# Wider products that carry the low-rank rows with the values, and the first outputs' load at the head of the last pair

## The reference

```
h = x @ W.T + b + 2 * (x @ A[i]) @ B[i]         # A: 1024 x 16, B: 16 x 1024, i per sequence
q, k, v = h @ w_q, h @ w_k, h @ w_v             # bs 8, 32 query heads, 8 key and value heads of 32
o = softmax(q k.T / sqrt(32)) v ;  x = x + o @ w_o
y = x @ weight[j].T                             # j per sequence
x = x + sum over the best 2 of 4 experts of gate * 4 * (y @ A_e.T) @ B_e.T
```

## Time and profile before

| | |
|---|---|
| runs | 1053.78, 1052.08, 1053.18 us |
| profiled execution | 1050.59 us, of it the span 1048.9 us |
| busy | PE 97%, PE weight loads 78%, DVE 60%, ACT 43%, POOL 22% |
| mean granted TensorE clock | 0.988 |
| weight folding ends, first pair begins | 162.5 us |
| score groups of step 0, pairs 1 to 4 | 183.5, 312.6, 447.0, 582.4 us |

### The profile page before, as it was taken

One profiled execution on the slowest core, in us unless ns is written; L12 is line 12 of the kernel. 1 busy time (PEld: TensorE's weight loads), 2 busy tenths in 40 slices (PEclk: granted clock), 3 DMA queues, 4 the chain that ended last, 5 costly groups with the idle time before them and its releaser, 6 DMA issues.

```text
span 1048.9 us, 17421 instructions
## 1 busy us (share of the span) xinstructions
PE 1013.4 (97%) x6934; PEld 820.2 (78%) x6934; DVE 633.5 (60%) x1071; ACT 449.5 (43%) x782; POOL 234.0 (22%) x224
## 2 busy tenths in 40 slices
PE   7999999999999999999999999999899999999997
PEld 6878787877678776787767787676589998988986
DVE  6562724667856578664776657654665655655653
ACT  5121223355754557554665556635422332323321
POOL 1000001123323233223332246643111111111100
PEclk9999999999999999999999999999999999999998
DMA  7030312111421124211232134453966756766531
GB/s 263 0 101 1 131 47 73 27 38 43 123 55 38 29 56 122 60 40 27 53 113 60 42 93 142 123 154 142 257 215 197 229 193 199 228 196 205 201 122 40
DMA packets 49888, 117.41 MB, mean 112 GB/s; under 512 B 7298, under 2 KB 26114, under 8 KB 45712
## 3 DMA queue, kind: packets, MB, share of 16 engines
q1 hardware_dynamic: 40080, 81.70, 26.4%
q0 software_dynamic: 9728, 34.61, 10.4%
HBM read 86.38 MB, written 18.89 MB: 100 GB/s over the span
## 4 chain that ended last, share of the span: by engine, by line
PE 90%; DMA 3%; DVE 3%; ACT 1%; SPq 1%; issue 1%; POOL 0%; ACTq 0%
PE psP L759 20%; PE psW L1043 17%; PE psF L254 11%; PE psG L1071 8%; PE psO L825 6%; PE psT L812 5%; PE psS L801 5%; PE psP L774 4%; PE psX L1286 3%; PE psO L829 2%; PE psY L1305 2%; PE psF L265 1%; DMA x_raw<-in_xT 1%; PE psM L836 1%; PE psP L740 1%; PE psP L742 1%
## 5 line engine op out<-in xcount | busy, mean ns | idle before, releaser
L673 DVE TENSOR_REDUCE nmax<-psS 128x2 f32<-128x512 f32 x256 | 164.5, 684 | 153.8 <-PE psS L801 152.1
L550 POOL TENSOR_TENSOR p_sum<-probs 128x512 f32<-128x512 f32 x128 | 167.6, 1310 | 372.6 <-ACT probs L600 372.3
L759 PE MATMUL psP<-x_hl,wq 128*128 128x512 f32 x960 | 235.1, 392 | 0.6 <-DVE q_stack L653 0.6
L759 PEld LDWEIGHTS psP<-x_hl,wq 128*128 128x128 f32 x960 | 175.2, 189 | 32.8 <-issue 0.8
L1043 PE MATMUL psW<-wq 128*128 128x256 f32 x1536 | 196.7, 283 | 1.6 <-DVE q_stack L653 1.2
L1043 PEld LDWEIGHTS psW<-wq 128*128 128x128 f32 x1536 | 190.3, 191 | 6.2 <-issue 1.3
L600 ACT ACTIVATE probs<-psT 128x512 f32<-128x512 f32 x256 | 139.2, 596 | 54.4 <-PE psT L812 53.9
L1052 ACT ACTIVATE cond_hi<-cond_raw 128x1024 fp32r<-128x1024 f32 x64 | 66.8, 1057 | 152.5 <-PE psG L1071 148.1
L1056 DVE TENSOR_TENSOR cond_lo<-cond_raw,cond_hi 128x1024 fp32r<-128x1024 f32 x64 | 78.3, 1235 | 89.1 <-ACT cond_hi L1052 89.0
L812 PE MATMUL psT<-q_stack,k_stack 98*128 98x512 f32 x256 | 90.1, 427 | 7.7 <-ACT probs L600 5.4
L653 DVE TENSOR_TENSOR q_stack<-psP,q_stack 32x512 fp32r<-32x512 f32 x128 | 87.8, 686 | 9.2 <-ACT q_stack L566 7.1
(11 more groups left out here) (122 smaller groups left out, 1252.8 us busy)
## 6 DMA issues: line engine op xcount, KB each, us to landing
cond_raw<-in_cond POOLq DMA_DIRECT2D x64, 512.0 KB, 4.1
x_raw<-in_xT SPq DMA_DIRECT2D x32, 256.0 KB, 3.9
q_stack<-q_stack SPq DMA_DIRECT2D x32, 256.0 KB, 3.1
o_scratch<-o_sb SPq DMA_DIRECT2D x64, 128.0 KB
o_raw<-rden_scratch SPq DMA_DIRECT2D x32, 256.0 KB, 5.4
o_raw<-o_scratch SPq DMA_DIRECT2D x8, 1024.0 KB, 8.8
x_sb<-in_xT SPq DMA_DIRECT2D x8, 1024.0 KB, 6.8
outT<-x_sb SPq DMA_DIRECT2D x32, 256.0 KB, 2.5
```

The source lines that it names most:

```text
L550: pool.tensor_tensor(p_sum[:, heads], probs[:, 0, heads], probs[:, 1, heads], ALU.add).then_inc(sum_done, 1)
L673: dve.tensor_reduce(nmax[:, n % 2, 2 * hp:2 * hp + 2, qt], psS[:, i % 2].rearrange("p (h k) -> p h k", h=2), AX.X, ALU.max, negate=True).t ...
L759: mm = pe.matmul(out, wq[:, i, w, k * P:(k + 1) * P], x[:, k, part], start=(k == 0 and n_ == 0), stop=False)
```

## The change

The low-rank factor A moves from `a_stack` into the moving side of the v products: `v_hi` holds for each k 32 columns of A (high and low half) of one sequence, 256 of the value weights and 32 of the other sequence, and a v unit's three products per k have 288, 272 and 256 columns. The 32 extra columns are x @ A per token; VectorE adds their two halves into `u_tok`, the unit "t" turns four such tiles with TensorE, and ScalarE and VectorE make `u_stack` from it. The values' own low-rank product can't be the v unit's last any more, so the units "r0" and "r1" multiply it into two further banks and VectorE adds it to `v_sb`, which is held twice. The blocks of the weights, `WORK` and `SEQ` are rearranged: all v units of a pair lie in steps 13 and 14 of the pair before. The x rows are split three in step 11 and five in step 12 by ScalarE, three in step 12 and five in step 13 by VectorE. The load of the first outputs is issued at the end of the step ahead of the last pair, multiplied in its step 0, and split in steps 1 and 2. Buffers are moved in SBUF for all of this, and the last tiles of the weight folding are taken out by two instructions each.

```diff
-BLOCKS = ["k0", "q0", "q1", "q2", "v0", "v1", "q3", "k1", "q4", "q5", "q6", "q7"]
+BLOCKS = ["k0", "q0", "q1", "q2", "q3", "k1", "q4", "q5", "q6", "q7", "v0", "v1"]
+VB = BLOCKS.index("v0")
+VC = NKV + 4 * R
+V0 = 2 * R
...
+                units = range(CB * j, CB * (j + 1))[:VB - CB * j]
+                ins = nc.scalar.activation(wq[:, units[0]:units[-1] + 1, 0, m * P:(m + 1) * P],
+                                           psF[:, bank(j, m), 0:P * len(units)].rearrange("p (u c) -> p u c", c=P), ACT.Copy)
+                if j == CHUNKS - 1:
+                    ins = nc.scalar.activation(v_hi[:, m, V0:V0 + NKV], psF[:, bank(j, m), P * len(units):512], ACT.Copy)
+                ins.then_inc(tile_hi, 1)
...
+                if j == CHUNKS - 1:
+                    ins = dve.tensor_tensor(v_lo[:, m], psF[:, bank(j, m), P * len(units):512],
+                                            f(v_hi[:, m, V0:V0 + NKV]), ALU.subtract)
+                ins.then_inc(tile_lo, 1)
...
 WORK = [
-    (["v0"], ["q2:0-4"]),
-    (["q2:4-6"], ["q2:6-8"]),
-    (["v1"], ["v2"]),
-    (["v3"], ["q3:0-4"]),
-    (["q3:4-8"], ["k1:0-4"]),
-    (["k1:4-8"], ["q4:0-3"]),
+    (["r0", "r1"], ["q2:0-3"]),
+    (["q2:3-6"], ["q2:6-8"]),
+    (["q3:0-2"], ["q3:2-5"]),
+    (["q3:5-8"], ["k1:0-2"]),
+    (["k1:2-4"], ["k1:4-6"]),
+    (["k1:6-8"], ["q4:0-3"]),
     (["q4:3-6"], ["q4:6-8"]),
     (["q5:0-3"], ["q5:3-5"]),
-    (["q5:5-8"], ["q6:0-3"]),
-    (["q6:3-6"], []),
-    (["q6:6-8"], ["q7:0-3"]),
-    (["q7:3-6"], []),
+    (["q5:5-8"], ["q6:0-2"]),
+    (["q6:2-4"], ["q6:4-6"]),
+    (["q6:6-8"], ["q7:0-2"]),
+    (["q7:2-4"], ["q7:4-6"]),
     (["q7:6-8"], []),
-    (["+u:0-4"], ["+u:4-8"]),
-    (["+k0"], ["+q0"]),
-    (["+q1:0-4"], ["+q1:4-8"]),
+    (["+v0:0-4", "+v1:0-4"], ["+v0:4-8", "+v1:4-8"]),
+    (["+v2", "+v3"], ["+t", "+k0"]),
+    (["+q0"], ["+q1"]),
 ]
-SEQ = ["u", "k0", "q0", "q1", "v0", "q2", "v1", "v2", "v3", "q3", "k1", "q4", "q5", "q6", "q7"]
+SEQ = ["v0", "v1", "v2", "v3", "t", "k0", "q0", "q1", "r0", "r1", "q2", "q3", "k1", "q4", "q5", "q6", "q7"]
 NS = len(SEQ)
-SEQ_DVE = [u for u in SEQ if u[0] != "v"]
-ND = len(SEQ_DVE)
+SEQ_ACT = [u for u in SEQ if u[0] != "r"]
+NA = len(SEQ_ACT)
+SEQ_QK = [u for u in SEQ if u[0] in "qk"]
...
+        def copy_t(p):
+            act.wait_ge(proj_done, unit(p, "t") + 1)
+            nc.scalar.activation(u_stack[0:32], psP[0:32, bank(p, "t")], ACT.Copy, scale=LORA_SCALE)
+            nc.scalar.activation(u_stack[32:64], psP[0:32, bank(p, "t")], ACT.Copy, scale=LORA_SCALE).then_inc(proj_act, 1)
...
-            if p:
-                act.wait_ge(pv_done, STEPS * p + c - 1)
-            nc.scalar.activation(v_sb[:, c, t % 2], psP[:, bank(p, f"v{t}"), 0:NKV].rearrange("p (g d) -> p g d", g=G),
+            if p >= 2:
+                act.wait_ge(pv_done, STEPS * (p - 1))
+            nc.scalar.activation(v_sb[p % 2][:, c, t % 2],
+                                 psP[:, bank(p, f"v{t}"), c * V0:c * V0 + NKV].rearrange("p (g d) -> p g d", g=G),
                                  ACT.Copy).then_inc(proj_act, 1)
...
-            for unit_ in evacuated(n, 0):
+            for unit_ in finished(n, 0):
                 evacuate(*unit_)
-            for unit_ in evacuated(n, 1):
-                if unit_[1][0] == "v":
+            for unit_ in finished(n, 1):
+                if unit_[1][0] in "vt":
                     evacuate(*unit_)
             if 2 <= n <= N + 1:
                 exp(n - 2, 2)
...
             if more and s == 9:
                 split_a_hi(act, p + 1)
             if more:
-                for k in {11: range(0, 6), 12: range(6, KT)}.get(s, ()):
+                for k in {11: range(0, 3), 12: range(3, KT)}.get(s, ()):
                     split_x_hi(act, p + 1, k)
-            for unit_ in evacuated(n, 1):
-                if unit_[1][0] != "v":
+            for unit_ in finished(n, 1):
...
-                dve.tensor_tensor(u_t[:], psP[0:32, bank(p, "u")], u_t[:], ALU.add).then_inc(proj_dve, 1)
-                dve.wait_ge(u_hi_done, p + 1)
-                dve.scalar_tensor_tensor(u_stack[64:96], u_t[:], LORA_SCALE, f(u_stack[0:32]),
-                                         ALU.mult, ALU.subtract).then_inc(u_lo_done, 1)
+            if u[0] == "v":
+                c, rows = j // 2, NKV * (1 - j // 2)
+                dve.wait_ge(proj_act, act_unit(p, u) + 1)
+                if p and j == 0:
+                    dve.wait_ge(proj_done, unit(p - 1, "t") + 1)
+                dve.tensor_reduce(u_tok[:, j, c], psP[:, bank(p, u), rows:rows + 2 * R].rearrange("p (h r) -> p r h", h=2),
+                                  AX.X, ALU.add).then_inc(proj_dve, 1)
+            elif u == "t":
+                dve.wait_ge(proj_act, act_unit(p, "t") + 1)
+                dve.scalar_tensor_tensor(u_stack[64:96], psP[0:32, bank(p, u)], LORA_SCALE, f(u_stack[0:32]),
+                                         ALU.mult, ALU.subtract).then_inc(proj_dve, 1)
+            elif u[0] == "r":
+                values = v_sb[p % 2][:, j].rearrange("p k g d -> p (k g d)")
+                dve.wait_ge(proj_done, unit(p, u) + 1)
+                dve.wait_ge(proj_act, act_unit(p, f"v{2 * j + 1}") + 1)
+                dve.tensor_tensor(values, values, psP[:, bank(p, u)], ALU.add).then_inc(proj_dve, 1)
...
                 maxima(n, 0)
                 maxima(n, 1)
             if more:
-                for k in {12: range(0, 6), 13: range(6, KT)}.get(s, ()):
+                for k in {12: range(0, 3), 13: range(3, KT)}.get(s, ()):
                     split_x_lo(dve, p + 1, k)
-            for unit_ in evacuated(n - 1, 1) if n else [(0, "q1")]:
-                if unit_[1] != "u":
+            for unit_ in finished(n - 1, 1) if n else [(0, "q1")]:
+                if unit_[1][0] in "qk":
+                    evacuate(*unit_)
+            for unit_ in finished(n, 0):
+                if unit_[1][0] not in "qk":
                     evacuate(*unit_)
             ahead.vector(dve, n, 0)
...
                 invert(dve, p - 1)
             if more and s == 9:
                 split_a_lo(dve, p + 1)
-            for unit_ in evacuated(n, 0):
-                evacuate(*unit_)
-            for unit_ in evacuated(n, 1):
-                if unit_[1] == "u":
+            for unit_ in finished(n, 0):
+                if unit_[1][0] in "qk":
+                    evacuate(*unit_)
+            for unit_ in finished(n, 1):
+                if unit_[1][0] not in "qk":
                     evacuate(*unit_)
             ahead.vector(dve, n, 1)
...
-                pe.wait_ge(proj_act, i + 1)
                 q, v = i // NS, SEQ[i % NS]
-                if v in SEQ_DVE:
-                    pe.wait_ge(proj_dve, dve_unit(q, v) + 1)
+                if v in SEQ_ACT:
+                    pe.wait_ge(proj_act, act_unit(q, v) + 1)
+                pe.wait_ge(proj_dve, i + 1)
...
+        def turn_rows(p):
+            free(p, "t")
+            pe.wait_ge(proj_dve, unit(p, "v3") + 1)
+            for t in range(TILES):
+                mm = pe.transpose(psP[0:32, bank(p, "t"), t * P:(t + 1) * P],
+                                  u_tok[:, t].rearrange("p c r -> p (c r)"), id_sb[:])
+            mm.then_inc(proj_done, 1)
         def low_rank_ready(p):
...
+            c, toks = t // 2, slice(t * P, (t + 1) * P)
+            if first == 0:
+                free(p, f"v{t}")
+                if t == 0:
+                    pe.wait_ge(a_lo_done, p + 1)
+            out = psP[:, bank(p, f"v{t}")]
+            hi_rows, lo_rows, lo_out = ((slice(V0, VC), slice(V0, VC - R), slice(0, NKV + R)) if c == 0 else
+                                        (slice(0, VC - V0), slice(R, VC - V0), slice(R, NKV + V0)))
+            for k in range(first, end):
+                if t == 0:
+                    pe.wait_ge(x_lo_done, KT * p + k + 1)
+                pe.matmul(out[:, 0:NKV + V0], x[:, k, 0, toks], v_hi[:, k, hi_rows], start=(k == 0), stop=False,
+                          skip_group_check=True)
+                pe.matmul(out[:, lo_out], x[:, k, 1, toks], v_hi[:, k, lo_rows], start=False, stop=False,
+                          skip_group_check=True)
+                mm = pe.matmul(out[:, c * V0:c * V0 + NKV], x[:, k, 0, toks], v_lo[:, k], start=False, stop=(k == KT - 1),
+                               skip_group_check=True)
+            if end == KT:
+                mm.then_inc(proj_done, 1)
...
+        def low_rank_v(p, c):
+            free(p, f"r{c}")
+            for t in range(2):
+                toks = slice(c * T + t * P, c * T + (t + 1) * P)
+                mm = pe.matmul(psP[:, bank(p, f"r{c}"), t * NKV:(t + 1) * NKV], u_stack[:, toks],
+                               b_stack[:, VB * P:(VB + 2) * P], start=True, stop=True)
+            mm.then_inc(proj_done, 1)
...
             if g == 0:
-                pe.wait_ge(proj_act, unit(p, f"v{2 * c + 1}") + 1)
+                pe.wait_ge(proj_dve, unit(p, f"r{c}") + 1)
```

(85 more changed lines are left out.)

141 lines of the change are left out of this document (64 added, 77 removed).

## The result

The changed kernel takes 1096.0 us in the median of four runs (1095.2 to 1099.2), the kernel before, beside it, 1052.6 (1050.6 to 1053.8): a ratio of 1.042, with an interval of 1.039 to 1.045. It is 43 us slower. The forecast was 24 us slower, 1077, and its range ended at 1087: the side was right, the size was not.

A forecast was written before the change was run, and what follows sets the result against it. The prediction took TensorE, busy 97% of the span, as the bound. Gains of 28.2 us and losses of 52.2 us gave +24.0 us, so 1077 us, with a range of 1057 to 1087.

The forecast's parts named there:

- products and filled parts: Per pair: fewer products on TensorE, -8.8 us in all, and empty parts of steps 9 and 11 filled, -5.7 us.
- waits and clock in step 12: Step 12: three waits for exponentials go, 5.4 us plus 1.7 us of clock each, -10.5 us.
- first outputs at the head: Last pair's head: moving the first outputs' load removes most of a maxima wait and its clock loss, -3.2 us.
- step 13, x row 3: Step 13: v0 waits 4.2 us, three times, for VectorE to split x row 3, +12.5 us.
- t: Step 14: transposes wait for VectorE's sum of v3, 1.9 us three times and 0.9 once, +6.6 us.
- r1: Step 0: r1 waits for q1's subtractions in its bank, about 4 us in each of four pairs, +16.1 us.
- half clock behind the new waits: Behind ten new TensorE waits the clock halves, losing 1.7 us each, +17 us.
- The three places: Waits at step 13 (+12.5 us), at t in step 14 (+6.6) and at r1 in step 0 (+16.1).
- Empty parts of steps: Steps 9 and 11, four pairs: each empty second part costs 0.7 us, so filling them gains 5.7 us.
- ten falls of 1.7 us: Half clock behind the new waits in step 13, step 14 and step 0 (3 + 3 + 4), +17 us together.

The follow-up runs named there:

- q0_first: Changed kernel with r/t banks, q7 evacuated late, v2/v3 copies first, products refilled, t between k0's halves, q0 evacuated before step 15's row maxima: 1047.4 us, ratio 0.993.
- before_filled: Kernel before the change, with only step 9's empty second part filled (q6 products in steps 8 and 9): 1053.1 against 1052.5 us, ratio 1.0004.
- refill: Changed kernel with steps 2 to 12 filled otherwise, q3 and q5 ending in second parts, units and their order unchanged: 1086.3 us.
- v_copy_first: Changed kernel with ScalarE's copies of v2 and v3 put ahead of its copy of the row maxima in step 14: 1083.7 us.
- q7_late: Changed kernel with q7 copied behind step 12's exponentials and x rows and subtracted behind step 13's x rows, when a next pair follows: 1081.8 us.
- x_three_k: Changed kernel with three k of v0 and v1 in step 13's first part and five in its second: 1089.9 us.
- r1_later: Changed kernel with r1 moved from step 0 to step 1: 1091.3 us.
- own_banks: Changed kernel with banks assigned by hand: r0 and r1 in q1's bank, moved to step 1, t in v3's bank: 1085.5 us.
- load_back: The q0_first kernel with the first outputs' load back in step 8 of the last pair, multiplied and split in steps 10 and 11: 1047.6 us, ratio 0.9961.

## Why the forecast missed

Against its own sum, by the profiled spans:

| step of the forecast | forecast | measured |
|---|---|---|
| products and filled parts | -14.5 | -11.4 (what the other rows leave of 44.7, and so with every small difference besides) |
| waits and clock in step 12 | -10.5 | -10.5 |
| first outputs at the head | -3.2 | -4.0 |
| step 13, x row 3 | +12.5 | +12.0 |
| t | +6.6 | +6.2 |
| r1 | +16.1 | +14.6 (15.2 less the 0.6 of before) |
| half clock behind the new waits | +17 | +21.7 |
| outputs and sums | 0 | +15.1 (16.2 less the 1.1 of before) |
| first scores of a pair (a wait put down to issue) | 0 | +1.0 |

**What held.** The three places, each to 1.5 us, were read from the order of instructions in the kernel before, and the wide products cost what the line through two widths said. Between the first scores of the second and third pair lie 149.8 us (335.09 to 484.86); less 13.9 us of waits and 7.6 of clock they are 128.3, and the kernel before, less its own wait and fall there, 134.4 - 1.7 - 1.7 = 131.0. The 2.7 us between are less than the forecast's 2.2 for products and 1.4 for filled parts. One price in its sum was wrong the other way: the four transposes of t take 0.36 us (461.26 to 461.62), not 0.84, so the products should give 2.7 by themselves. By these differences nothing is left for the filled parts. They are rough, though: `q0_first`, with the same products filled in otherwise, comes out at 131.8 - 1.9 = 129.9, so how much of the 2.7 us each of the two gave stays open.

**The step that failed is "Empty parts of steps".** It counted what the products gain in the part they enter, 0.7 us, and not what the part they leave had covered. `before_filled` shows this alone, at step 9: +0.5 us for three steps in place of -0.7. In the changed kernel the same waits stand twice a pair, 0.65 us and 0.28 for the sum, 7.4 us in all, where the forecast had 5.7 gained and nothing lost. About as much, 8.2 us, comes from step 4, which no term of the forecast holds: q3 ends a step earlier than its place in `q_stack` allows, and the outputs wait 1.77 us and their sum 0.29, four times. The rest of the 16.2 us are two more sums. `refill`, which moves nothing but these products, takes all twelve waits for exponentials away and gains 9.7 us; eight of the sums' short waits stay.

**The clock was mis-sized.** The forecast took ten falls of 1.7 us. All ten came, but six lost 1.7 us and four 2.6 to 3.2: behind four of the seven waits of 3.8 us and more the clock stayed at its lower level about twice as long. Counted over the time in which TensorE had work at that level this is 21.7 us. v0's wait of 4.0 us shows both, in the second pair (it ends at 439.69) and in the third (588.14); the columns are those of the windows above:

```profile
438.00:442.00 4.00, 2.31 (x10) 2.31 (x11) 4.00 (x7) 1.77 (x4) 0.52 (x1) 0.54 0.16 44
442.00:446.00 4.00, 4.00 (x33) 2.42 (x33) 0.05 (x1) 0.00 (x1) 0.00 (x0) 0.60 0.00 0
...
590.00:594.00 4.00, 4.00 (x38) 2.74 (x37) 0.50 (x1) 0.54 (x2) 0.00 (x0) 0.76 0.00 0
594.00:598.00 4.00, 4.00 (x33) 3.91 (x32) 2.43 (x6) 2.21 (x6) 1.29 (x1) 1.00 0.29 87
```

Why the same wait costs one or the other stays open. The Trainium skill ("TensorE: Matmul & The Clock Gate", section "HAM oscillation — how this bites in real kernels") wants no gaps above a length that t's 1.8 us waits stay under; the trace disagrees, with 1.7 us lost behind each of the three.

**A wait can move.** Taking one wait away gained at least its full length where what was waited for came earlier (`v_copy_first`, 12.4 us for 5.4 of waits, `q7_late`, 14.2 for 12.0, both with clock won back), and about half or less where the products only came later (`x_three_k`, 6.1 for 12.0, `r1_later`, 4.8 for 15.2), since the next product stood in front of the same VectorE instructions. The Trainium skill ("Perfetto Trace Analysis", section "Matmuls") wants groups to rotate through PSUM banks so that taking out one overlaps the next one's products. The trace agrees, and shows what that asks of the next group: r0's 0.24 us cannot cover a way out of 4 us, and with r in the bank of q1 while q2 runs in the other the wait is gone (`own_banks`).

Whether the load at the head gains anything once the waits are mended stays open; `q0_first` and `load_back` cannot be told apart.

## What to carry to other kernels

Count for each product that moves what it covered where it stood, not only what it fills where it goes: on an engine that takes its work in order, the wait appears behind the place it left. With two banks in turn, ask of every short unit what covers the way out of the unit ahead of it, and give it a bank of its own turn rather than a later place. Take a wait away by making its cause earlier; moving the one who waits mostly moves the wait.

## What was unexpected of the hardware

In the thirteen profiles the products of the second stage (projections, scores, outputs) wait 136 times for 0.85 us or more. None of the 24 waits below 1.3 us had a fall of the clock behind it. Of the 59 from 1.3 to 1.9 us 29 had one, of the 16 from 1.9 to 3.1 us 13. All 37 of 3.8 us and more had one, 17 of them losing 1.5 to 1.7 us and 20 of them 2.2 to 3.2. The outputs' wait of 1.77 us in step 4 stands 24 times, in the changed kernel and five others: 5 times it had a fall behind it, in the changed kernel never, in `r1_later` in the second pair alone. The same pause in the same program place can thus cost nothing, or its own length again.
